# Key parts ahead of query parts in the stacking order, query pieces of 896 bytes, and a reordered ramp in a cross-attention and expert kernel

## What is computed

```python
# x [16, 112, 256], ctx [16, 375, 256], mask [16, 375]
q = heads(layernorm(x) @ Wq.T + bq); k = heads(ctx @ Wk.T + bk); v = heads(ctx @ Wv.T + bv)
scores = where(mask == 0, -1e9, q @ k.T / sqrt(16))
x = x + (softmax(scores) @ v) @ Wo.T + bo
flat = layernorm(x)                       # 1792 rows
w, e = top_k(softmax(flat @ router_w), 2); w = w / sum(w)
x = x + sum over both choices of w * (silu(flat @ w1[e]) @ w2[e])
```

## Time and profile before

| | before |
|---|---|
| median of 3 runs | 467.08 us |
| the profiled execution | 465.15 us, its span 463.3 us |
| TensorE matmul busy | 414.2 us (89%) |
| VectorE busy | 340.2 us (73%) |
| ScalarE busy | 277.9 us (60%) |
| GpSimd busy | 224.4 us (48%) |

### The profile page before, as it was taken

The page is one execution under the profiler, slowest core; times in us unless marked ns, Lnnn a source line. Parts: engine busy times, 40 slices in busy tenths (PEclk is TensorE's granted clock), DMA queues, the critical chain, the costliest instruction groups (busy, mean ns, idle before and its releaser), DMA issues.

```text
span 463.3 us, 10813 instructions
## 1 busy us (share of the span) xinstructions
PE 414.2 (89%) x4219; PEld 385.6 (83%) x4219; DVE 340.2 (73%) x699; ACT 277.9 (60%) x374; POOL 224.4 (48%) x254
## 2 busy tenths in 40 slices
PE   7867899999998999999999997589989999999810
PEld 6746798998897998899998996579989999999810
DVE  7965677887787877788878868966686676777545
ACT  4547655656665566656554553447777777778600
POOL 6754642024431344421312573755787787876420
PEclk9888999999999999999999998579999999999975
DMA  7794527774768766667660149922222222332169
GB/s 209 190 214 128 133 73 157 154 185 117 170 146 180 163 143 154 147 139 151 131 129 11 48 150 373 317 59 70 80 81 84 88 91 81 92 82 69 45 224 296
DMA packets 50692, 64.32 MB, mean 139 GB/s; under 512 B 18834, under 2 KB 39587, under 8 KB 50643
## 3 DMA queue, kind: packets, MB, share of 16 engines
q1 hardware_dynamic: 44338, 50.40, 43.4%
q0 software_dynamic: 4096, 11.13, 8.2%
q10 hardware_dynamic: 2208, 2.12, 1.4%
HBM read 30.13 MB, written 9.28 MB: 85 GB/s over the span
## 4 chain that ended last, share of the span: by engine, by line
PE 76%; DVE 8%; DMA 6%; issue 3%; ACT 3%; SPq 1%; POOL 1%; ACTq 0%; POOLq 0%; DVEq 0%
PE ps L1533 39%; PE ps L1596 12%; PE ps L1613 9%; PE ps L1627 9%; DMA k_stack<-k_lo 2%; PE ps L1900 2%; PE ps L1640 2%; DMA mask_scratch<-mask_rows 1%; DMA y_rows<-y_out,slot_of_row 1%; DMA y_back<-y_rows 1%; DVE neg_max L1095 1%; PE ps L1696 1%; DMA keep_scratch<-keep_all 1%; PE ps L1652 1%; DMA mask_all<-mask 1%
## 5 line engine op out<-in xcount | busy, mean ns | idle before, releaser
L1095 DVE TENSOR_REDUCE neg_max<-ps 112x1 f32<-112x376 f32 x256 | 133.6, 545 | 45.2 <-PE ps L1596 40.5
L829 ACT ACTIVATE probs<-ps 125x1344 f32<-125x1344 f32 x64 | 82.7, 1293 | 43.8 <-PE ps L1613 38.6
L1596 PE MATMUL ps<-k_stack,q_stack 98*112 98x376 f32 x256 | 86.6, 372 | 8.1 <-issue 3.6
L602 POOL TENSOR_TENSOR k_lo<-k_f,k_hi 128x752 fp32r<-128x752 f32 x16 | 28.9, 1808 | 118.0 <-ACT k_hi L803 118.0
L760 POOL DMA_INDIRECT rows<-xn_rows,token_of_row x42 | 55.2, 1315 | 18.9 <-issue 12.5
L1596 PEld LDWEIGHTS ps<-k_stack,q_stack 98*112 98x112 f32 x256 | 44.8, 177 | 21.0 <-DVE neg_max L1095 10.6
L768 POOL DMA_INDIRECT y_rows<-y_out,slot_of_row x42 | 47.3, 1126 | 25.8 <-ACT y_out L1022 14.5
L1613 PE MATMUL ps<-q_stack,k_stack 100*125 100x224 f32 x384 | 52.5, 272 | 0.0
L1613 PEld LDWEIGHTS ps<-q_stack,k_stack 100*125 100x125 f32 x384 | 50.6, 188 | 0.6 <-ACT probs L829 0.5
L1533 PE MATMUL ps<-w_hi,h_hi 128*128 128x256 f32 x168 | 48.7, 290 | 1.6 <-issue 1.6
L1533 PE MATMUL ps<-flat_t_hi,w_hi 128*128 128x256 f32 x168 | 47.5, 283 | 1.9 <-DVE flat_t_lo L1420 1.9
(11 more groups left out here) (213 smaller groups left out, 1024.8 us busy)
## 6 DMA issues: line engine op xcount, KB each, us to landing
k_stack<-k_hi SPq DMA_DIRECT2D x32, 376.0 KB, 5.8
w_all<-w SPq DMA_DIRECT2D x2, 4096.0 KB, 18.9
k_stack<-k_lo SPq DMA_DIRECT2D x16, 376.0 KB, 7.1
ctx_raw<-ctx_t SPq DMA_DIRECT2D x32, 187.5 KB, 6.4
q_stack<-attn_t_hi SPq DMA_DIRECT2D x64, 56.0 KB
y_back<-y_rows SPq DMA_DIRECT2D x14, 256.0 KB, 4.7
x_rows_sb<-x_rows SPq DMA_DIRECT2D x4, 448.0 KB, 5.1
x<-x_tiles SPq DMA_DIRECT2D x7, 256.0 KB, 3.8
```

What stands on the lines that cost most here:

```text
L602: pool.tensor_tensor(kl[:, :, :], kf[:, :, :], kh[:, :, :].bitcast(F32), ALU.subtract)\
L829: act.activation(pf[j % 2][:, :, :], ps[0:CT, BK_ST:BK_ST + KT, 0:4 * S], ACT.Exp).then_inc(pf_ready, 1)
L1095: dve.tensor_reduce(neg_max[:, s:s + 1], ps[0:S, BK_MAX + s % 2, 0:CP], AX.X, ALU.max, negate=True).then_inc(max_read, 1)
L1596: pe.matmul(ps[0:S, BK_MAX + a, 0:CP], qs[b.ring][0:R_MAX, q, S * a:S * (a + 1)], ks[b.ring][0:R_MAX, q, :], start=True, stop=True).then_i ...
```

## The change

Five things change.

1. The queries' layout: both halves of two neighbouring dimensions of a batch lie next to each other, so a row's piece of a query copy is 2 x 112 numbers (896 bytes) where it was 2 pieces of 448. The query stack is `[P, 2, HALF, S]` instead of `[P, HALF, 2 * S]`, so that the destination of a copy is contiguous too. `quad_scores` therefore reads its moving operand with a gap between its two runs of 112. `query_low` and `first_query_low` become two instructions each, and the maxima's columns are permuted.
2. SyncE's turn: keys, then queries, then mask, where it was queries, mask, keys. The waits for the ring's last user stand ahead of the keys.
3. SyncE's ramp: the mask's write to HBM goes ahead of the loads of Wv and of the third group of rows; the first batch's keys and queries go ahead of the wait for that write and of the mask; the second batch's queries and mask go ahead of the load of the fourth group, and its keys between that and the context loads.
4. ScalarE's and VectorE's ramp: `attn_weight(3)` and the router's part ahead of `normalise_x(2)` and `key_high(second)`; `q_high(1, 0)` ahead of `x_std(3)` and the exponential's table; `q_high(1, 1)` ahead of `normalise_x(3)`; the scaling of bq ahead of `attn_weight_low(1)`.
5. GpSimd: the third batch's `key_low` goes from turn 0 into the ramp, between `query_low(2)` and `query_low(3)`.

```diff
-        qh = [th[:, :, SG * g:SG * (g + 1)] for g in range(NG)]
-        ql = [tl[:, :, SG * g:SG * (g + 1)] for g in range(NG)]
+        qh, ql = (x.rearrange("p a (b k n) -> p b a k n", k=KD, n=S) for x in (th, tl))
...
-        qs = [sb(f"q_stack{p}", [P, HALF, 2 * S], F32R) for p in range(RINGS - 1)]
+        qs = [sb(f"q_stack{p}", [P, 2, HALF, S], F32R) for p in range(RINGS - 1)]
...
-                queue.dma_start(qs[b.ring][row + c:row + PARTS * DK:PARTS, :, S * a:S * (a + 1)].bitcast(F32),
-                             src[half:half + P // 2, :, S * b.n:S * (b.n + 1)].bitcast(F32))\
-                    .then_inc(done, 16)
+                queue.dma_start(qs[b.ring][row + c:row + PARTS * DK:PARTS, a, :, :].bitcast(F32),
+                                src[half:half + P // 2, b.n // 2, b.n % 2, :, :].bitcast(F32)).then_inc(done, 16)
...
             def turn(b):
                 if has(b.after(2)):
-                    stack_queries(b.after(2))
                     if b.n == 0:
                         sp.wait_ge(xt_done, NG)
+                    else:
+                        sp.wait_ge(st_done, QUADS * b.n)
+                    stack_keys(b.after(2))
+                    stack_queries(b.after(2))
                     stack_mask(b.after(2))
-                    stack_keys(b.after(2))
...
             load_keep(0, slice(0, 2))
+            sp.wait_ge(mask_rows_ready, 1)
+            sp.dma_start(mask_scratch, m_rows[:, :, :].bitcast(F32)).then_inc(mask_written, 16)
             load_weight(2, wv_t)
             load_rows(2)
-            sp.wait_ge(mask_rows_ready, 1)
-            sp.dma_start(mask_scratch, m_rows[:, :, :].bitcast(F32)).then_inc(mask_written, 16)
             load_weight(3, wo_t)
             sp.dma_start(rw_raw[:, :, :], router_w.rearrange("k p n -> p k n")).then_inc(rw_in, 16)
+            stack_keys(first)
+            stack_queries(first)
             sp.wait_ge(mask_written, 32)
             stack_mask(first)
-            stack_keys(first)
-            stack_queries(first)
-            load_rows(3)
-            load_ctx(first.after(2))
             sp.wait_ge(filled, 4)
             stack_queries(second)
             stack_mask(second)
+            load_rows(3)
             stack_keys(second)
+            load_ctx(first.after(2))
             load_ctx(first.after(3))
...
             query_low(2)
+            key_low(first.after(2))
             query_low(3)
...
             x_std(2)
-            normalise_x(2)
-            key_high(second)
             attn_weight(3)
             act.wait_ge(rw_in, 16)
             act.copy(rw[:, :, 0:E], rw_raw[:, :, :]).then_inc(rw_ready, 1)
+            normalise_x(2)
+            key_high(second)
             x_high(2)
             values(first, True)
             values(first, False)
+            q_high(1, 0)
             x_std(3)
             act.activation(root_c[:, :], eps_c[:, :], ACT.Exp)
-            q_high(1, 0)
+            q_high(1, 1)
             normalise_x(3)
-            q_high(1, 1)
...
+            dve.wait_ge(bias_in, 48)
+            dve.tensor_scalar(bq_c[:, :], bq_c[:, :], DK ** -0.5, None, ALU.mult).then_inc(const_set, 1)
             attn_weight_low(1)
             x_low(0)
-            dve.wait_ge(bias_in, 48)
-            dve.tensor_scalar(bq_c[:, :], bq_c[:, :], DK ** -0.5, None, ALU.mult).then_inc(const_set, 1)
...
-                                         qs[b.ring][0:ROWS, 2 * j + q, :], start=True, stop=True)
+                                         qs[b.ring][0:ROWS, :, 2 * j + q, :], start=True, stop=True)
```

More of the change, by code:

```diff
@@ L225, in xattn_moe_kernel @@
         first_queries = 4 * (B * D + 2 * KD * SG)
-        qs.append(sb(f"q_stack{RINGS - 1}", [P, HALF, 2 * S], F32R))
+        qs.append(sb(f"q_stack{RINGS - 1}", [P, 2, HALF, S], F32R))
         assert cursor["at"] <= xr_at + 4 * 2 * GB * D, "the last query stack lies where the first two groups of x were"
@@ L441, in stack_queries @@
             def stack_queries(b):
-                if not early(b, RINGS):
-                    sp.wait_ge(st_done, QUADS * (b.n - RINGS + 1))
                 if b.n == RINGS - 1:
@@ L448, in stack_queries @@
                 sp.wait_ge(qh_ready, KD * (g + 1))
-                stack_part(sp, b, 0, th, q_stacked[b.ring])
-                stack_part(sp, b, 2, th, q_stacked[b.ring])
+                stack_part(sp, b, 0, qh, q_stacked[b.ring])
+                stack_part(sp, b, 2, qh, q_stacked[b.ring])
                 if not early(b, 1):
                     sp.wait_ge(ql_ready, g + 1)
-                    stack_part(sp, b, 1, tl, q_stacked[b.ring])
+                    stack_part(sp, b, 1, ql, q_stacked[b.ring])
             def stack_keys(b):
@@ L466, in stack_max @@
                     sp.wait_ge(mx_ready, 2 * b.n + r + 1)
-                    sp.dma_start(qs[b.ring][R_MAX + r:R_MAX + r + 1, :, :].bitcast(F32)
-                                 .rearrange("p q (a n) -> p (q a) n", a=2), mx[:, r, :].bitcast(F32))\
+                    sp.dma_start(qs[b.ring][R_MAX + r:R_MAX + r + 1, :, :, :].bitcast(F32)
+                                 .rearrange("p a q n -> p (a q) n"), mx[:, r, :].bitcast(F32))\
                         .then_inc(mx_stacked[b.ring], 16)
@@ L620, in query_low @@
                 pool.wait_ge(qh_ready, KD * (g + 1))
[L621 to L626, removed]
+                for b in range(2):
+                    last = pool.tensor_tensor(ql[:, 2 * g + b, :, :, :], qf[:, b, :, :, :],
+                                              qh[:, 2 * g + b, :, :, :].bitcast(F32), ALU.subtract)
+                last.then_inc(ql_ready, 1)
+            fills = [(qs[0][R_MASK:ROWS, :, :, :], 1.0), (vx[0][:, :, :, DK:VC], 1.0),
+                     (qs[1][0:R_MASK, :, :, :], 0.0), (qs[1][R_MASK:ROWS, :, :, :], 1.0), (vx[1][:, :, :, DK:VC], 1.0),
+                     (qs[2][0:R_MASK, :, :, :], 0.0), (qs[2][R_MASK:ROWS, :, :, :], 1.0)]
             assert len(fills) == N_FILLS
@@ L644, in _ @@
             pool.wait_ge(ql_ready, 1)
-            stack_part(pool, first, 1, tl, first_low_stacked)
+            stack_part(pool, first, 1, ql, first_low_stacked)
             fill(range(1, 5))
@@ L664, in turn @@
             def turn(b):
-                if has(b.after(2)):
+                if has(b.after(2)) and b.n:
                     key_low(b.after(2))
@@ L1094, in maxima @@
                         dve.wait_ge(maxt_done, b.n)
-                    dve.tensor_reduce(neg_max[:, s:s + 1], ps[0:S, BK_MAX + s % 2, 0:CP], AX.X, ALU.max,
+                    head = HALF * (s % 2) + s // 2
+                    dve.tensor_reduce(neg_max[:, head:head + 1], ps[0:S, BK_MAX + s % 2, 0:CP], AX.X, ALU.max,
                                       negate=True).then_inc(max_read, 1)
@@ L1126, in _ @@
             dve.wait_ge(const_set, 1)
[L1127 removed]
+            dve.memset(qs[0][0:R_MASK, :, :, :].bitcast(F32), 0.0).then_inc(const_set, 1)
             def x_stats(g):
@@ L1159, in first_query_low @@
                 dve.wait_ge(qh_ready, t + 1)
-                ins = dve.scalar_tensor_tensor(out=ql[0][:, t, :], in0=ps[:, (2, BK_OUT)[t], 0:SG],
-                                               scalar=bq_c[:, t:t + 1], in1=qh[0][:, t, :].bitcast(F32),
-                                               op0=ALU.add, op1=ALU.subtract)
+                for b in range(2):
+                    ins = dve.scalar_tensor_tensor(out=ql[:, b, :, t, :], in0=pairs(ps[:, (2, BK_OUT)[t], 0:SG])[:, b, :, :],
+                                                   scalar=bq_c[:, t:t + 1], in1=qh[:, b, :, t, :].bitcast(F32),
+                                                   op0=ALU.add, op1=ALU.subtract)
                 if t == KD - 1:
@@ L1595, in head_scores @@
                     a, q = s % 2, s // 2
-                    pe.matmul(ps[0:S, BK_MAX + a, 0:CP], qs[b.ring][0:R_MAX, q, S * a:S * (a + 1)],
+                    pe.matmul(ps[0:S, BK_MAX + a, 0:CP], qs[b.ring][0:R_MAX, a, q, :],
                               ks[b.ring][0:R_MAX, q, :], start=True, stop=True).then_inc(smax_done, 1)
```

10 lines of the change are left out of this document (6 added, 4 removed).

## The result

The changed kernel takes 460.53 us (median of 4 runs, 460.38 to 461.67) against 467.07 us of the kernel before beside it (466.53 to 467.87): ratio 0.9864, 95% interval 0.9843 to 0.9885, that is 5.4 to 7.3 us faster. The forecast was 461.6. The profiled execution took 460.38 us with a span of 458.5. Lines of the changed kernel lie up to 7 further down than before: L1596 is now L1603, L1613 L1620, L1627 L1634, L1533 L1540, L415 L414.

The account below looks back on a forecast made before the run. TensorE was taken to set the time, with holes from late keys in the turns and hand-overs bounding the ramp. Turns 3.6, first turn 0.7 and ramp 1.2 sum to 5.5 us, from 467.08 to 461.6 us; range 459.3 to 465.0.

Parts of the forecast that it names:

- Late keys: Attention turns: five TensorE holes behind the marks are keys landing late; keys ahead of queries removes all, 3.58 us.
- The queries' margin: Attention turns: with keys first, the last byte lands at about 75.4, 1.3 us before heads want it.
- R2: Slower rival, turns: queries land last; strong form 492 us, chance 0.03; mild form 463 to 465 us, chance 0.06.
- Pieces: Turns: query pieces of 896 bytes instead of 448 save zero; up to 0.57 us of DMA time off the path.
- by bytes, even cheaper per byte when small: DMA in turns: packet time follows bytes, from 183 ns per key packet of 2.3 KB and 24 ns per 448-byte query packet.
- The gap in the moving operand: quad_scores in turns: reading two runs of 112 with a gap costs zero; other bound 5.8 us.
- R3: Rival, quad_scores: the gap in the moving operand costs up to 5.8 us, 467.4 us at its end; chance 0.05.
- The first turn: First turn: key_low ahead of query_low(3) shortens TensorE's 0.91 us hole; 0.7 us won, bounds 0 and 0.91.
- The ramp: Before the turns: x_stats(3) at 32.4, project_queries(2) at 35.5 instead of 36.67; gain 1.2 us, bounds +2.3 and -1.0.
- The sum: Whole kernel: 3.6 + 0.7 + 1.2 = 5.5 us gained, 461.6 us off the median; chance 0.58.
- R1: Rival: turns gain, ramp doesn't, as rows of x land at 34 us or later; 462.8 to 463.8 us, chance 0.13.
- R4: Rival, turns: the holes are not the keys' and remain; gain only 1.9 us, 465.2 us, chance 0.05.

## Why the prediction was right, point by point

**Late keys.** Right in cause and size. The forecast was five holes, 3.58 us; twelve turns became 3.82 us shorter, the order alone gives 0.81%, undone it costs 0.65%. Reading a piece "issue" by issue and landing of the transfer that is needed last held, and more closely than the prediction put it: in the profile of before the low key parts of the five disturbed turns landed 7.3, 7.4, 6.8, 7.1 and 7.2 us after their issue, and each of the five holes ends some 0.1 us after such a landing.

**The queries' margin.** Right: no turn waits for them, so neither form of R2 came. The working had them land with 1.3 us to spare at the worst; they bear the context's 375 KB in front as well, and with 1 MB in front the mask behind them comes too late.

**Pieces.** On the path I took zero and measured 0.1% with an interval over both signs. Off the path "by bytes, even cheaper per byte when small" was wrong. Both means from the earlier trace rows mix packet sizes (the 576 packets hold 64 of 4 bytes, the 390 some of 4 and 448 bytes), and the keys' were taken with the engines at a share of 0.89. Measured by themselves, pieces of 448 bytes take 25.5 ns and of 896 bytes 40.5: twice the size costs 1.59 times as much, so the small piece is the dearer one per byte, and the prediction's remark that the trace agrees with copies within on-chip memory not suffering doesn't hold for these pieces. A turn saves 0.25 us of all engines (bounds were 0 and 0.57), hidden as forecast. The gap in the moving operand costs nothing: six matmuls of quad_scores take 0.65 us in the chain of both kernels, the median record 272 ns (before 271). R3 is out.

**The first turn.** The hole fell from 0.91 to 0.33 us, 0.58 where I took 0.7. What is left of it still ends with GpSimd's ctx_lo (53.32 to 55.12), which now waits 1.02 us for ScalarE's high part. The step missed something: key_low's move is not only a gain of its own but a condition of the new order, since SyncE's queue now stands at GpSimd's k_lo with queries and mask behind. Without the move the second turn's heads wait another 0.61 us, in one execution. I had named what is queued behind that wait for an ordinary turn and not for turn 0.

**The ramp.** x_stats(3) at 32.15 (forecast 32.4), project_queries(2) at 35.43 (35.5), gain there 1.24 us (1.2). Up to the maxima's transpose it grew to 1.54. Yet two profiles of the kernel before differ by 0.87 us in the first mark (61.75, 60.88), and the ramp alone gave 1.0 us by the medians; so the agreement to a tenth is partly luck. First heads came 2.8 us sooner, where I thought 1 to 2; as argued, that didn't matter.

**The sum.** 5.5 forecast, 6.5 by the medians (interval 5.4 to 7.3), and 4.8 between the two profiles. The profiles differ less because the first of before had the higher clock in routing; at the last mark of the turns they are 5.9 us apart. R1 didn't come; R4 is refuted by the run with the order alone. What remains open is where the missing 1 us lies. The prediction looked for it in more holes in ordinary runs of before: those seen sum to 3.6, 2.3, 4.0, 3.8 and 2.2 us in five executions with the old order, which doesn't bear that out. The order was worth 3.8 us alone and 3.0 on top of the rest, where the forecast had 3.6; ramp, first turn and pieces together gave 3.3 us (0.71%, interval 2.1 to 4.4), where it had 1.9. So the records point to the second group, but the intervals are too wide to show it, and the forecast's nearness to the measured time is in part luck.

## What to carry to other kernels

When the trace puts a hole at a matmul down to no releaser, add the landing time of the last transfer that the matmul needs to its issue: if the sum meets the hole's end in every case, suspect the queue's order and change it alone; here the heavy transfers belonged first, as soon as their data existed, and the light ones behind. Before a wait is moved up in a queue, look for the one turn, mostly the first, in which its producer runs late. A load that is moved back to make room is the next bound: it is worth trying each idle stretch of the issuing queue for it, and asking each time whose bytes it shares the DMA engines with; here the rows right behind the fills, with the third context moved up too, took the kernel from 1.4% to 2.6% under the one before. And a stand of TensorE is paid twice where the granted clock is lower behind it, as the 24 matmuls of 6.29 us against 4.56 show.

## What the runs showed of the hardware

Copies within on-chip memory took 25.5 ns for a packet of 448 bytes and 40.5 ns for one of 896 bytes while queries went nearly alone (57 and 45 ns per 1000 bytes), and a packet of 4 bytes took 9 ns. With the queues full (237 to 242 us of before) a key packet of 3008 bytes took 245 ns in the mean and 116 at the least, so a mean taken there is no price by bytes. A VectorE subtraction with two operands in on-chip memory took 1.93 us where GpSimd's k_lo ran (VectorE at 27.21, k_lo from 26.79 to 28.59 in the kernel before) and 0.68 us where GpSimd filled a buffer with a constant (VectorE at 22.14, fills from 19.70 to 22.95). The Trainium skill, SBUF — State Buffer, Who interferes with whom, says that a VectorE instruction with two inputs in on-chip memory contends with a GpSimd instruction that reads this memory and not with one that only writes it; the two rows agree. The granted clock in the routing stage was 0.84 over 42 us in one execution of the kernel before and 0.74 in another, and the stage was 1.3 us longer in the second.
